# Delta layer of an eight-layer kernel: logits turned before keys, key copies on ScalarE, softmax before the scores, values and Gram blocks stored earlier in SyncE's order

## The reference, cut to what matters

```python
q = _short_conv(hidden_states @ Wq.T, conv_q).reshape(b, l, H, DK)
k = _short_conv(hidden_states @ Wk.T, conv_k).reshape(b, l, H, DK)
v_direct = _short_conv(hidden_states @ Wv.T, conv_v).reshape(b, l, H, DV)
beta = jax.nn.sigmoid(hidden_states @ Wb.T)
...
A = jnp.where(tri_strict, -(kbc @ jnp.swapaxes(kc, -1, -2)), 0.0)
T = solve_triangular(M, jnp.broadcast_to(eye, M.shape), lower=True)
...
delta_out = tp(_delta_rule_chunkwise(tp(q), tp(k), tp(v_direct), jnp.transpose(beta, (0, 2, 1))))
local_s = _fir(v_direct, fir_s)
local_m = _fir(v_direct, fir_m)
local_l = _fir(v_direct, fir_l)
logits = jnp.einsum('bld,hpd->blhp', hidden_states, gate_w) + gate_b
probs = jax.nn.softmax(logits / temp, -1)
probs = probs * (1.0 - 5.0 * eps) + eps
o = probs[..., 0:1] * local_s + probs[..., 1:2] * local_m + probs[..., 2:3] * local_l + probs[..., 3:4] * delta_out + probs[..., 4:5] * v_direct
```

## Time and profile before

| | |
|---|---|
| median of 3 runs | 4527.42 us (4522.19 to 4541.84) |
| profiled execution, its own time | 4525.58 us |
| its span | 4523.7 us |
| busy over the span | PE 84%, DVE 56%, POOL 45%, ACT 42% |
| first 600 us | PE busy 455.12, DVE 374.81, ACT 176.32, POOL 245.26 us |

### The profile page before, as it was taken

How to read it: one execution, slowest core, us unless ns; L and a number is a source line. 1 busy time by engine, 2 the same in 40 slices (tenths; PEclk the granted TensorE clock), 3 DMA queues, 4 the chain that set the end, 5 groups by cost and what they waited for, 6 DMA issues and landing times. The chain is left out here.

```text
span 4523.7 us, 70653 instructions
## 1 busy us (share of the span) xinstructions
PE 3818.0 (84%) x26056; PEld 2648.4 (59%) x26088; DVE 2533.4 (56%) x4540; ACT 1896.2 (42%) x3440; POOL 2013.6 (45%) x2061
## 2 busy tenths in 40 slices
PE   7687787799999349948999799688888888999995
PEld 3547664467676249924554455366666666656663
DVE  6666453454554662247777322588888887312223
ACT  4132233333333112226666322588888886112222
POOL 6313462222322126632342111399999998332223
PEclk9798998999999669968999899899999999899997
DMA  5747541200000639945544200111111112822224
GB/s 192 246 140 226 151 108 64 75 10 10 19 10 10 219 87 296 276 123 148 157 138 135 84 33 24 51 52 52 50 50 48 45 45 64 265 90 45 46 46 133
DMA packets 334072, 459.67 MB, mean 102 GB/s; under 512 B 71222, under 2 KB 245750, under 8 KB 329606
## 3 DMA queue, kind: packets, MB, share of 16 engines
q1 hardware_dynamic: 311094, 424.27, 30.5%
q0 software_dynamic: 22512, 30.36, 3.6%
q10 hardware_dynamic: 128, 0.52, 0.0%
HBM read 314.54 MB, written 140.51 MB: 101 GB/s over the span
## 5 line engine op out<-in xcount | busy, mean ns | idle before, releaser
L3565 POOL TENSOR_TENSOR mamba_hC<-mamba_h_t,mamba_cb 128x512 f32<-128x512 f32 x512 | 675.3, 1344 | 73.3 <-DVE mamba_h_t L3078 64.3
L3078 DVE TENSOR_TENSOR_SCAN mamba_h_t<-mamba_dA,mamba_pB 128x512 f32<-128x512 f32 x512 | 596.3, 1206 | 121.1 <-PE mamba_pB L3456 50.7
L3456 PE MATMUL mamba_pB<-ident,mamba_dBT 128*128 128x128 f32 x2048 | 327.4, 284 | 58.1 <-DVE mamba_h_t L3078 51.9
L3254 ACT ACTIVATE mamba_dA<-mamba_delta,mamba_a_neg 128x512 f32<-128x512 f32 x512 | 356.3, 713 | 17.9 <-DVE mamba_h_t L3078 17.2
L3456 PEld LDWEIGHTS mamba_pB<-ident,mamba_dBT 128*128 128x128 f32 x2048 | 239.1, 144 | 195.0 <-issue 103.8
L3465 PE MATMUL mamba_pY<-ident,mamba_hC 128*128 128x128 f32 x2048 | 318.8, 280 | 15.2 <-POOL mamba_hC L3565 14.2
L1911 POOL TENSOR_SCALAR mqa_prob<-mqa_prob,mqa_rinv 128x128 f32<-128x128 f32 (+3 forms) x256 | 136.2, 532 | 425.4 <-DVE mqa_rinv L1687 424.4
L2350 DVE TENSOR_REDUCE mha_nmax<-mha_pM 128x1 f32<-128x384 f32 (+3 forms) x352 | 215.7, 635 | 106.6 <-PE mha_pM L2658 103.5
L3245 ACT ACTIVATE mamba_dBT<-mamba_eT,mamba_b_t 128x512 f32<-128x512 f32 x384 | 273.5, 713 | 0.1
L1501 POOL DMA_INDIRECT top_sum<-top_y,top_xg x71 | 110.3, 1554 | 351.7 <-ACT top_y L1290 341.5
L3465 PEld LDWEIGHTS mamba_pY<-ident,mamba_hC 128*128 128x128 f32 x2048 | 246.3, 144 | 23.7 <-POOL mamba_hC L3565 22.9
(11 more groups left out here) (622 smaller groups left out, 8897.3 us busy)
## 6 DMA issues: line engine op xcount, KB each, us to landing
expert_w<-in_L_ffn_W SPq DMA_DIRECT2D x48, 1024.0 KB, 5.9
delta_shared<-delta_w SPq DMA_DIRECT2D x64, 576.0 KB, 5.1
mamba_cb<-mamba_c SPq DMA_DIRECT2D x128, 256.0 KB, 3.2
mha_qkT<-mha_parts_d SPq DMA_DIRECT2D x96, 256.0 KB, 5.0
expert_w<-in_L_ffn_W SPq DMA_DIRECT2D x48, 256.0 KB, 6.5
top_w<-in_L_ffn_w SPq DMA_DIRECT2D x24, 512.0 KB, 10.3
delta_w<-delta_wst SPq DMA_DIRECT2D x17, 576.0 KB, 3.3
top_slots<-top_y SPq DMA_DIRECT2D x1, 9159.0 KB, 36.7
```

The costliest lines, as they stand in the source:

```text
L3078: nc.vector.tensor_tensor_scan(h_t[:, n % RH, :], dA[:, n % RA, :], pB[n % 2][:, :], 0.0, ALU.mult, ALU.add).then_inc(z["scan_ready"], 1)
L3254: nc.scalar.activation(dA[:, n % RA, :], delta[:, a % 2, ct, :], ACT.Exp, scale=a_neg[:, ct, s:s + 1])\
L3456: last = nc.tensor.transpose(pB[n % 2][:, tok(t)], dBT[:, r % RS, t, ct * P:(ct + 1) * P], c.ident[:, :])
L3565: nc.gpsimd.tensor_tensor(hC[:, n % RO, :], h_t[:, n % RH, :], cb[:, r % RC, :], ALU.mult)\
```

## The change

1. **SyncE, first half.** Matrices 16 to 27 are stored later: 16 to 19 behind the values, 20 and 21 behind the load of `vn`, and 22 to 31 behind beta (before: 28 to 31). Two buffers serve from matrix 20 on (before: from 25).
2. **SyncE, both halves.** `vn` is loaded after the second of four groups of Gram blocks, not after the fourth.
3. **TensorE.** The logits are turned ahead of the keys, into banks 4 and 5 (before: 2 and 3), and no longer wait for the last Gram copy.
4. **ScalarE** copies the keys (before: VectorE), with the exponential in their middle. The root for the scores stands behind `regroup(1)`.
5. **VectorE** finishes the softmax ahead of its waits for the Gram stores and `lt`.

```diff
-        place = [g % 5 if g < 25 else (g - 25) % 2 for g in range(FG)]
+        place = [g % 5 if g < 20 else (g - 20) % 2 for g in range(FG)]
...
                     if hf == 0:
-                        for g in range(8, FG - 4):
+                        for g in range(8, 16):
                             store_table(g)
...
+                    if hf == 0:
+                        for g in range(16, 20):
+                            store_table(g)
                     for i in range(NCH // 4):
                         n = NCH // 4 * hf + i
...
-                    sp.wait_ge(z["v_st"], 16 * HB * CH // R * (hf + 1))
-                    if hf:
-                        sp.wait_ge(z["o_st"], 16 * hf)
-                    else:
-                        for i in range(2, 5):
-                            sp.wait_ge(w_st[i], 16 * place.count(i))
-                    sp.dma_start(vn[:, :, :], runs_of(v_d, hf)).then_inc(z["vn_in"], 16)
+                        if i == 1:
+                            sp.wait_ge(z["v_st"], 16 * HB * CH // R * (hf + 1))
+                            if hf:
+                                sp.wait_ge(z["o_st"], 16 * hf)
+                            else:
+                                for k in range(2, 5):
+                                    sp.wait_ge(w_st[k], 16 * place.count(k))
+                            sp.dma_start(vn[:, :, :], runs_of(v_d, hf)).then_inc(z["vn_in"], 16)
+                            if hf == 0:
+                                for g in range(20, 22):
+                                    store_table(g)
...
                     if hf == 0:
-                        for g in range(FG - 4, FG):
+                        for g in range(22, FG):
...
-                    for i in range(NCH // 2):
-                        n = NCH // 2 * hf + i
-                        dve.wait_ge(z["kr_ps"], n + 1)
-                        if n == NCH // 2:
-                            dve.wait_ge(z["kr_kept"], 32)
-                        nc.vector.tensor_copy(kr[:, 2 * i:2 * i + 2, :].rearrange("p n d -> p (n d)"), bank[6 + n % 2][:, :])\
-                            .then_inc(z["kr_ready"], 1)
                     for s in range(4):
                         dve.wait_ge(z["gl_ps"], 4 * hf + s + 1)
-                        ps, some = bank[2 + s % 2], slice(8 * (s % 2), 8 * (s % 2) + 8)
+                        ps, some = bank[4 + s % 2], slice(8 * (s % 2), 8 * (s % 2) + 8)
...
-                    dve.wait_ge(z["g_st"], 64 * NCH // 4 * (hf + 1))
-                    nc.vector.memset(vp[:, :, :, 0:PAD * HB], 0.0).then_inc(z["pads"], 1)
...
+                    dve.wait_ge(z["soft_exp"], hf + 1)
+                    link(nc.vector.tensor_reduce(gred[:, :], flat, AX.X, ALU.add))
...
+                    nc.vector.tensor_tensor(rqk[:, 0, :, :], rqk[:, 0, :, :], gate[:, 1, :, :, 3], ALU.mult)\
+                        .then_inc(z["soft_done"], 1)
+                    dve.wait_ge(z["g_st"], 64 * NCH // 4 * (hf + 1))
+                    nc.vector.memset(vp[:, :, :, 0:PAD * HB], 0.0).then_inc(z["pads"], 1)
                     dve.wait_ge(z["lt_in"], 16 * (hf + 1))
...
-                    dve.wait_ge(z["soft_exp"], hf + 1)
-                    link(nc.vector.tensor_reduce(gred[:, :], flat, AX.X, ALU.add))
...
-                    act.wait_ge(z["lt_sum"], hf + 1)
-                    nc.scalar.activation(rs[:, :, :], rs[:, :, :], ACT.Sqrt).then_inc(z["lt_root"], 1)
-                    act.wait_ge(z["soft_sub"], hf + 1)
-                    nc.scalar.activation(gate[:, :, :, :, :], gate[:, :, :, :, :], ACT.Exp).then_inc(z["soft_exp"], 1)
+                    for i in range(NCH // 2):
+                        n = NCH // 2 * hf + i
+                        act.wait_ge(z["kr_ps"], n + 1)
+                        if n == NCH // 2:
+                            act.wait_ge(z["kr_kept"], 32)
+                        if i == NCH // 4:
+                            act.wait_ge(z["soft_sub"], hf + 1)
+                            nc.scalar.activation(gate[:, :, :, :, :], gate[:, :, :, :, :], ACT.Exp).then_inc(z["soft_exp"], 1)
+                        nc.scalar.activation(kr[:, 2 * i:2 * i + 2, :].rearrange("p n d -> p (n d)"), bank[6 + n % 2][:, :],
+                                             ACT.Copy).then_inc(z["kr_ready"], 1)
...
                     regroup(0)
                     regroup(1)
+                    act.wait_ge(z["lt_sum"], hf + 1)
+                    nc.scalar.activation(rs[:, :, :], rs[:, :, :], ACT.Sqrt).then_inc(z["lt_root"], 1)
                     filter_in(0)
...
                     pe.wait_ge(z["logit_ready"], base + HB)
+                    pe.wait_ge(z["vr_ready"], NCH // 2 * (hf + 1))
+                    for s in range(4):
...
+                                last = nc.tensor.transpose(bank[4 + s % 2][:, i * GX:(i + 1) * GX],
...
                     for i in range(NCH // 2):
                         n = NCH // 2 * hf + i
...
-                    pe.wait_ge(z["g_ready"], NCH // 2 * (hf + 1))
-                    for s in range(4):
...
-                                last = nc.tensor.transpose(bank[2 + s % 2][:, i * GX:(i + 1) * GX],
```

36 lines of the change are left out of this document (17 added, 19 removed).

## The result

| | before | after |
|---|---|---|
| median of 4 runs each, same chip | 4529.2 us (4522.19 to 4541.84) | 4560.4 us (4550.46 to 4561.36) |
| ratio, 95% interval | | 1.0062 [1.0045, 1.008], so 20 to 36 us slower |
| profiled execution, its span | 4525.58, 4523.7 us | 4550.46, 4548.4 us |

The change makes the kernel slower by 0.6%; the forecast was 4538 us with a range up to 4550. In the first half the mechanism is the one forecast, GpSimd's rounds behind the large loads, but it costs more than the sum said; the second half loses where a small gain stood.

A forecast was written before the change was run, and what follows sets the result against it. It took a chain of DMAs, issued in order by SyncE, to bound the gap between projections and filters; 4525.58 + 12.6 - 1.5 = 4536.7, the runs' median 1.84 above, so 4538 us; range 4519 to 4550.

The forecast's parts named there:

- The rival with the ring starting with beta: Half one: ring starts at about 148 instead of 157.25; with half two -14.8 us, so 4513; chance 0.10.
- The slow rival: Half one: every matrix store lands in 9.0 instead of 2.8 us behind other traffic; time 4563; chance 0.07.
- Part two: SyncE, half one: after stores 16 to 19 and half the Gram stores, `vn` goes out at about 127, 11.7 us earlier.
- Part three: SyncE's queue behind `vn`, half one: `lt` goes out at 142, 2 us later; stores 22 and 23 land by 148.4.
- the rival (`lt` at 134, +3.3): Half one: stores not held by the large loads, costing +3.3 instead of +12.6 us; time 4529; chance 0.17.
- Part four: GpSimd, half one: matrices 24 to 31 in rounds of 5.2 us from 148.4; matrix 31 built at 168.9, +12.6 us.
- its high end of +18.5: Half one: matrix rounds start at 151 and take 6.3 us each, so matrix 31 is built at 174.8.
- Part seven: SyncE, half two: `vn` earlier, sharing time with the remaining Gram stores; ring starts at 378.1 against 379.59, -1.5 us.
- the ends of -6 and +0.5: Half two's bounds for the ring's shift in us: -6 with all of `vn` hidden, +0.5 at the other end.
- Parts five and six: VectorE's earlier softmax (4.6 us a half) and ScalarE's key copies with TensorE's reordering: all covered, cost 0.
- The sum: Whole kernel: +12.6 us in half one and -1.5 in half two on 4525.58, giving 4536.7.
- high ends: Upper bounds of both halves' terms: +18.5 and +0.5, together +19 us, 4546 by the median.

The follow-up runs named there:

- e1_stores: Kernel before with only matrices 16 to 31 stored where the change stores them and two buffers from matrix 20; 4547.99 us, 1.0034.
- e2_vn_early: Kernel before with only the load of `vn` moved after the second of four groups of Gram stores, both halves; 4536.67 us, 1.0015.
- e8_again: The changed kernel once more, unedited, for its time and a second profile; 4552.88 us, 1.0058 to before.
- e3_engines: The changed kernel's TensorE, ScalarE and VectorE with SyncE's order and buffers as before; 4539.46 us, 1.0006.
- e9_order_b: Changed kernel's engines, three ring loads ahead of values, matrix 31 inside the ring, beta behind `lt`, ScalarE's root behind filter inputs, `vn` behind all Gram stores; 4516.83 us, 0.9972.
- e10_order_vn: e9_order_b with the load of `vn` after the second group of Gram stores in both halves; 4516.38 us, 0.9963.
- e7_beta: Kernel before with beta's stores and the load of `bs` moved ahead of `vn` in both halves; 4538.86 us, 1.0025.

## Why the prediction was wrong

**The forecast's mechanism holds in the first half.** GpSimd idle from 100.1 to 125.7 (said: about 99 to 122), waits of 0.46 us between the last rounds, TensorE's wait laid to the ring, no wait for ScalarE in half two: all are in the rows. The rival with the ring starting with beta would have needed matrix 31 before 156.27; it was built at 175.50. The slow rival, with rounds of 9.0 us landing, is not what happened either, although the time (4560) is near its 4563: the rounds took 5.34 us. (That 4563 also counts four rounds where the sum has three; with three it is 4557.)

**Part two is the step that failed in the first half**: "Four issues of stores 16 to 19 at 0.37 us ... end at 120.9". The price came from a lone load at 138.74. The four stores took from 119.54 to 124.72, 5.2 us, not 1.5: behind eight value stores an issue of one takes some 1.3 us on average (1.22 for the first, 3.92 for the other three), and so again in e1_stores (1.17 and 3.92). The Gram half then took 6.84 instead of 5.2, and the values 9.42 instead of 10.65. So `vn` went out 21.7 us behind the last value copy where I had 18.3. Of the 5.3 us by which the sum fell short in this half, 3.4 arise here. The second half is the control: without matrices between, `vn` follows the start of the values by 16.1 us, against 21.7 in the first.

**Part three** held in the first half: from `vn` to `lt` 15.6 us where I had 15, because there I had let the queue's 9.5 us and the Gram stores' 5.2 add. From `lt` to the landing of 22 and 23 it was 7.2, where I had 6.4. The rule of the Trainium skill, page "DMA: Bandwidth & Descriptors", section "Queues, rings and completion order", that each DMA engine consumes descriptors in ring order, agrees with these rows: stores 20 and 21, issued right behind `vn`, landed 1.5 us and more behind it, and the rival (`lt` at 134, +3.3) fell. That a store thus waits for the load is my conclusion; the section itself adds that a later descriptor may finish its write before an earlier one, which these rows don't show.

**Part four** measured 20.9 us from the start of matrix 24 to the end of 31, against 20.5: right. Part two to four together: matrix 31 was built at 175.50 instead of 168.9, of which 1.35 us is the later end of this execution's value copies. The ring's shift is +17.9 instead of +12.6, just inside its high end of +18.5.

**Part seven is the step that failed in the second half; it has the wrong sign**: "Taking 372.5, `lt` and beta land at 377.5 and the ring starts at 378.1 ... -1.5 us". I let the load of `vn` (6.0 us) and the rest of the Gram stores (5.5) share their time. They add: from `vn` to `lt` it was 11.7 us, against 6.0 + 5.5 = 11.5, where I had 9.6. With these 2.1 us, `vn` 1.2 us later than I had it and 0.7 more from `lt` to the ring, the ring comes 2.5 us later than before and not 1.5 sooner, outside the ends of -6 and +0.5. e2_vn_early shows the same by itself (+3.4), and e8_again repeats it (+1.6). It was inconsistent to add the same two things in half one and to let them overlap in half two.

**Parts five and six** are right: e3_engines is 1.0006, and the softmax's new place brought the first product 3 us forward (4.6 in part five) on a path that TensorE then held.

**The sum** by the measured rows would have been +17.9 + 2.5 = 20.4 on 4525.58, so 4546; by two profiles of each kernel the second layer starts 20.1 us later (713.6 against 693.5), and the profiled executions' own times differ by 21.4 (mean of 4550.46 and 4539.19 against mean of 4525.58 and 4521.27). The medians of the runs differ by 31 us in the first comparison and 26 in the second, with intervals of 20 to 36 and 18 to 35. The rows agree with the lower end of both; whether the executions without a profile lose some 5 us more, or that is scatter, these runs leave open. Nor is the agreement of 20.4 and 20.1 exact: of the 20.1, 1.6 us lie ahead of the last value copy of half one, where nothing was changed. That `vn` early costs 7 us by ratio and 5 by the rings of e2_vn_early (1.8 + 3.4) leaves the same small rest. So of the 22 us between the forecast of 4538 and the measured 4560, the rows show 9.3: 5.3 in half one and 4.0 in half two. The cause of the other 13 stays open; the first comparison's interval is wide enough to hold the rows' 20 us, so they may be scatter.

**The range** ended at 4550, part of the way from the 4546 of the terms' high ends to the slow rival's 4563. Those high ends gave +19; the measured terms gave +20.4, 4548 by the median of before. That lies inside the range; the median of the runs does not, by the part that stays open.

## What to carry to other kernels

When a load is issued ahead of stores that a later load waits for, count the load and the stores one after the other, not beside each other: in each of the eight halves measured here the later load went out 11.4 to 16.2 us behind the early one, where it was 1.3 to 1.4 in the old order, and an early start is worth something only if what it was ahead of is not wanted first. Before a producer's stores are moved behind something else, count its free buffers: from the moment they run out it makes one round of build and landing per pair, and each piece left unbuilt is paid there. A load whose data have long been there is the first candidate to be moved ahead. Here an order with three loads of the ring ahead of the values, and with the last matrix no longer ahead of the ring, was 13 us faster than before (e9_order_b), while the change was 26 to 31 slower. What each of the moves in that order is worth was not measured.

## What was not expected of the hardware

- **The price of an issue depends on what is ahead of it in the queue.** A store of a matrix (576 KB) behind eight value stores took some 1.3 us to issue on SyncE's queue, on average of four, two behind the load of `vn` 0.91 together. Eight Gram stores took 5.8 to 6.8 us with only stores ahead of them (e1_stores 5.78, e2_vn_early's first eight 5.79, after 6.84 and 6.56), 9.4 to 10.5 with the 2048 KB load ahead (e2_vn_early 9.93 and 10.46, after 9.63 and e8_again 9.41 in half two, e10_order_vn 9.74), and 12.69 and 13.27 with the load and two matrices ahead.
- **A load issued behind others lands as late as they do.** The ring's first loads of 576 KB, right behind `vn` and `lt`, landed in 12.2 us (e7_beta, half two), against 5.5 for the same three loads of before, which went out 9.7 us behind `lt` and not 0.5. In e7_beta `vn` and `lt` themselves landed 8.3 and 10.3 us after their issue.
- **Distances between later layers scatter.** From the second layer to the top layer the same kernel gave 3381.5 and 3373.2 us in two profiles, and even the last stretch of the delta layer, unchanged, varied between 222 and 229.6 us from kernel to kernel, so only the stretch itself tells where a change of this size has gone, and the interval over many runs what it is worth.
